# Taking the four key blocks of a causal attention in the order 0, 3, 1, 2

## What is computed

```python
q = q * cos + _rotate_half(q) * sin
k = k * cos + _rotate_half(k) * sin
scores = jnp.einsum('bqhd,bkhd->bhqk', q, k) / jnp.sqrt(jnp.float32(D))
causal = jnp.tril(jnp.ones((T, T), dtype=bool))
scores = jnp.where(causal, scores, jnp.float32(-1e+30))
p = jax.nn.softmax(scores, axis=-1)
y = jnp.einsum('bhqk,bkhd->bqhd', p, v).reshape(B, T, C)
```

## Time and profile before

| | |
|---|---|
| timed runs, median of 3 | 347.4 us (345.73, 347.4, 354.85) |
| the profiled execution | 344.2 us; its span in the profile 342.4 us |
| PE busy | 317.1 us (93%) |
| DVE busy | 248.9 us (73%) |
| ACT busy | 216.5 us (63%) |
| POOL busy | 127.7 us (37%) |
| causal attention, steps 0 to 31 | about 107 to 187 us |

### The profile page before, as it was taken

One profiled execution on the slowest core, in us unless ns is written; L12 is line 12 of the kernel. 1 busy time (PEld: TensorE's weight loads), 2 busy tenths in 40 slices (PEclk: granted clock), 3 DMA queues, 4 the chain that ended last, 5 costly groups with the idle time before them and its releaser, 6 DMA issues.

```text
span 342.4 us, 6803 instructions
## 1 busy us (share of the span) xinstructions
PE 317.1 (93%) x2270; PEld 221.3 (65%) x2270; DVE 248.9 (73%) x766; ACT 216.5 (63%) x641; POOL 127.7 (37%) x183
## 2 busy tenths in 40 slices
PE   8799989998989999997999998998999899999886
PEld 2348778664544333354544998995678687878675
DVE  4988875884889999988352563379787867888476
ACT  1488885374466755564378664764776576676995
POOL 3455563110732444403231360410685525545400
PEclk9999999999999999998799999999999999999999
DMA  7590000086752520090002003100100000000002
GB/s 210 192 278 5 2 0 2 9 264 173 208 190 72 138 74 3 11 351 15 2 17 71 2 23 101 50 0 0 56 17 17 1 2 0 3 0 0 2 0 64
DMA packets 21881, 22.47 MB, mean 66 GB/s; under 512 B 3894, under 2 KB 18646, under 8 KB 21846
## 3 DMA queue, kind: packets, MB, share of 16 engines
q1 hardware_dynamic: 18982, 16.78, 17.0%
q10 hardware_dynamic: 2352, 4.20, 3.8%
q0 software_dynamic: 512, 1.05, 1.0%
HBM read 14.22 MB, written 7.60 MB: 64 GB/s over the span
## 4 chain that ended last, share of the span: by engine, by line
PE 57%; DVE 17%; ACT 13%; issue 5%; POOL 4%; DMA 3%; SPq 0%; ACTq 0%; POOLq 0%
PE PS L1388 51%; PE PS L1442 5%; DVE PS L873 5%; ACT big L1176 5%; ACT big L1364 3%; POOL big L529 2%; DVE big L691 2%; DMA big<-in_A_WkT 2%; DVE big L716 2%; ACT big L1306 1%; DMA XN<-scr_y,pos 1%; ACT big L1150 1%; DVE XN L668 1%; POOL big L531 1%; DVE mraw L705 1%
## 5 line engine op out<-in xcount | busy, mean ns | idle before, releaser
L1388 PE MATMUL PS<-big 128*128 128x128 f32 (+10 forms) x592 | 94.6, 311 | 9.1 <-DVE mB L873 4.1
L1388 PEld LDWEIGHTS PS<-big 128*128 128x128 f32 (+3 forms) x592 | 56.4, 151 | 42.9 <-DVE mB L873 21.3
L529 POOL TENSOR_TENSOR big<-big,urec 128x1024 f32<-128x1024 f32 x24 | 45.6, 1898 | 60.2 <-DVE urec L723 45.5
L1176 ACT ACTIVATE big<-big 128x154 f32<-128x154 f32 x192 | 60.5, 318 | 10.9 <-DVE big L691 5.6
L873 DVE CUSTOM_DVE_ANT_0 PS<-PS,later 128x128 f32<-128x128 f32 (+3 forms) x128 | 59.9, 516 | 8.8 <-PE PS L1388 7.6
L1306 ACT ACTIVATE big<-PS 128x1024 f32<-128x1024 f32 (+3 forms) x64 | 42.8, 701 | 31.1 <-PE PS L1388 31.1
L1150 ACT ACTIVATE big<-PS 128x1280 f32<-128x1280 f32 (+2 forms) x30 | 32.3, 1087 | 27.0 <-PE PS L1442 24.5
L1388 PE MATMUL PS<-kkC,XT 128*128 128x462 f32 (+1 forms) x96 | 36.0, 511 | 2.2 <-DVE big L716 2.2
L517 POOL TENSOR_TENSOR rstd<-ve,minus_half 128x4 f32<-128x4 f32 (+2 forms) x13 | 13.2, 1016 | 61.8 <-DVE ve L663 61.8
L1176 ACT ACTIVATION_READ_ACCUMULATOR big<-big 128x1 f32 x192 | 36.1, 188 | 0.0
L1388 PEld LDWEIGHTS PS<-vwCm,big 128*128 128x128 f32 x256 | 30.9, 192 | 3.9 <-ACT big L1150 1.3
(11 more groups left out here) (193 smaller groups left out, 507.0 us busy)
## 6 DMA issues: line engine op xcount, KB each, us to landing
scr_qk<-big SPq DMA_DIRECT2D x12, 384.0 KB, 3.3
big<-scr_qk SPq DMA_DIRECT2D x16, 288.0 KB
big<-in_wv ACTq DMA_DIRECT2D x1, 2048.0 KB, 8.0
scr_x<-zrow SPq DMA_DIRECT2D x2, 448.0 KB, 6.4
scr_y<-big SPq DMA_DIRECT2D x2, 448.0 KB, 3.5
X<-in_x ACTq DMA_DIRECT2D x2, 256.0 KB, 3.4
big<-in_A_WoT ACTq DMA_DIRECT2D x1, 512.0 KB, 4.7
cw<-in_C_Wk SPq DMA_DIRECT2D x1, 512.0 KB, 5.3
```

The lines of the kernel that those rows point to most:

```text
L529: pool.tensor_tensor(pn[:, 0:GH * P].rearrange("p (h k) -> p h k", h=GH), Pt[u % 3][:, :, 0:KM], r.to_broadcast([P, GH, KM]), ALU.mult).th ...
L1176: i = act.activation(Pt[u % 3][:, h, :], Pt[u % 3][:, h, :], ACT.Exp, accum_out=usum[:, u % 3, h:h + 1])
L1388: return pe.matmul(o, lhsT, rhs, start=start, stop=stop)
```

## The change

The key blocks of each group are taken in the order 0, 3, 1, 2. Everything that went by kt as a place in the group (the first block, which starts the accumulation and waits; the last, which ends it) now goes by `at`, the place; everything that went by kt as a block (widths, slices) goes by `KEY_ORDER[at]`.

```diff
+        KEY_ORDER = (0, 3, 1, 2)
...
             for n in range(B * 4 * QT * 2):
                 s, pair = divmod(n, 2)
-                w = T - P * (s % QT)
+                w = T - P * KEY_ORDER[s % QT]
...
             def outputs(s):
 
-                bg, kt = divmod(s, QT)
+                bg, at = divmod(s, QT)
+                kt = KEY_ORDER[at]
...
-                if kt == 0 and bg:
+                if at == 0 and bg:
                     pe.wait_ge(yg_ready, bg)
                 for j in range(4):
                     i = mm(PS[32 * j:32 * j + 32, AV_BANK, kt * P:T], vaug[:, b, kt, 4 * g + j, :],
-                           PTb[:, 4 * ((s + 1) % 2) + j, 0:T - kt * P], start=kt == 0, stop=kt == QT - 1)
+                           PTb[:, 4 * ((s + 1) % 2) + j, 0:T - kt * P], start=at == 0, stop=at == QT - 1)
...
-                g, kt = divmod(step, QT)
+                g, at = divmod(step, QT)
+                kt = KEY_ORDER[at]
                 w = T - kt * P
-                if kt == 0:
+                if at == 0:
                     pe.wait_ge(m_ready[s // QT % 2], 16 * 3 * (s // QT // 2 + 1))
```

## The result

The kernel with the order 0, 3, 1, 2 takes 1.0061 times as long as before, with an interval of 1.0037 to 1.0085. This ratio leaves out the executions in which TensorE's clock was low for long (10 of 22 with the change, 3 of 22 before); the medians of all executions are 350.88 us (347.23 to 361.97) against 346.92 us (344.46 to 354.85), a ratio of 1.0114, and without those executions they are 348.5 against 346.6. A second comparison on another chip gave 1.0060 (1.0031 to 1.0088), with 345.86 us against 343.83 us. So the change costs some 2.1 us of 345 (0.0060 x 345), where the forecast was 350.2 us, 2.8 more than before. The range, 344.7 to 353.6 us, held the result, and it lies within the 2% that was given 91 in 100. The path behind the number was not all as forecast, and its errors partly offset each other.

What follows compares the result with a forecast made beforehand. PE and DVE, both near full, bound the first sequence; PE alone bounds steps 17 to 20. Terms 1.3 + 0 + 0.4 + 1.1 = 2.8 us, added to 347.4, gave 350.2 us; range 344.7 to 353.6.

Steps and rivals of the forecast that it cites:

- place 0: First step of a first-sequence group (kt 0): O 0.64 for 0.42, hidden by the mask; cost 0, or 0.21 uncovered.
- places 1 and 2: Second and third steps of a first-sequence group: kt 3 for kt 1, gain 0; kt 1 for kt 2, cost 0.12.
- place 3: Last step of a first-sequence group: O of kt 1, 0.85 for 0.64, right before the next S; cost 0.21.
- first sequence: Four groups, each 0.33 us longer: 1.3 us in all, bounds 0.4 and 2.2.
- steps 16 to 20: Start of the second sequence: PE is the bound and its sums of S and O stay the same; 0.
- steps 20 to 27: Second sequence, forecast as steps 21 to 27: longer S of step 23 and O of step 22 behind the logits; +0.4.
- steps 28 to 31: End of the attention: wider last steps and ACT's weight copies delay the last O; +1.1 us, bounds 0.3 and 1.4.
- the three signs: Group repeats in 9.5 us or less; clock row has another number of low slices; stage after step 31 changes length.
- Place 1: Second step of a first-sequence group, kt 3 for kt 1: S 0.24 shorter, O waits for the mask; gain 0.
- the clock stays up: Rival at step 21's wait: the stall no longer brings the clock's fall, 3.4 us come back, 346.8 us; 10 in 100.
- The second fall: Rival in steps 24 to 31: TensorE's clock falls once more, 3.4 us added, 353.6 us; 12 in 100.

Runs made afterwards that it cites:

- the control: The kernel before, unchanged, timed and profiled again beside itself; ratio 1.0016 (0.9986 to 1.0046).
- the first sequence alone: Against the kernel before: order 0, 3, 1, 2 in the four groups of the first sequence only; 344.06 us, 1.0016 (0.9989 to 1.0042).
- the whole change: The changed kernel as it is, order 0, 3, 1, 2 in both sequences, compared again with the kernel before; 345.86 us, 1.0060 (1.0031 to 1.0088).

## Why the prediction came out as it did

| term | forecast | measured | |
|---|---|---|---|
| place 0, a group | 0 | +0.07 | by DVE's copy, not named in the prediction |
| places 1 and 2, a group | 0 + 0.12 | +0.11 | |
| place 3, a group | +0.21 | +0.21 | |
| first sequence | 4 x 0.33 = 1.3 | 3 x 0.39 = 1.2 | group 0 costs nothing |
| steps 16 to 20 | 0 | +0.35 | |
| steps 20 to 27 | +0.4 | +0.83 + 0.11 = +0.94 | |
| steps 28 to 31 | +1.1 | +0.76 | |
| sum at the same clock | 2.8 | 3.24 | bounds were 0.7 and 4.1 |
| the clock | 0 (rival: -3.4) | about -1 | in executions without a long fall |

The median of 350.88 lies near the forecast of 350.2 by luck: the forecast is for an execution without a long fall of the clock, and those have a median of 348.5. The base of the forecast was high for such executions as well, 347.4 where they have 346.6. What can be held against the forecast is the difference, 2.8 for a measured 2.1, and the terms above. Of the three signs that were to show the prediction wrong, the first did not come (9.85 us, not 9.5 or less). The second did: the clock row has one low slice in place of two, but so has the control, so it is a matter of the execution. The third, the length behind step 31, was met in a small way only (155.3 for 155.6 and 155.8), apart from the profile taken with the result.

**The first sequence: size right, mechanism named wrongly.** The step that failed is "that O waits for the mask, which does not depend on it". O of kt 0 waits for DVE's copy of the last group's outputs (`yg_ready`); the runs without the masks and with a short copy show it. The two end 0.13 us apart, the trace names the mask, and the prediction took it at its word, although the kernel has `pe.wait_ge(yg_ready, bg)` in plain sight at that very place, in the diff even; the list of waits ahead of the prediction lacks it too. The sum survived by luck: the copy depends on the change only weakly, and the error of 0.07 in each of three groups was less than the 0.33 wrongly charged for group 0. Place 1, gain 0, held for a similar reason: the copy does not come earlier for a narrower S. PE's ring product ahead of O does, 2.93 behind S in place of 3.12, and PE then waits 0.24 us for the copy. (The 0.24 of the prediction's place 1 should have been 2 x (0.17 - 0.07) = 0.20 by its own prices.)

**Steps 16 to 20: the step that failed is "the sums are the same", so 0.** PE's work is the same, 10.5 to 10.6 us busy, but it is no longer without a gap. The S of step 17 is now 0.43 shorter (before, the four matmuls of 384 took 4 x 0.17, now 4 x 0.06 of 128), while O of kt 0 behind it stays where the copy puts it: 3.80 behind S of step 16, where it was 3.73. PE waits 0.25 us there, and the other 0.10 of the 0.35 stands as busy time. It is the argument made for place 1 of the first sequence, that a gain ahead of a fixed wait is lost, and it was not carried over: where work moves from before a fixed wait to behind it, an equal sum is a loss.

**Steps 20 to 27: mis-sized, 0.94 for 0.4.** What was forecast is there: step 23 takes 1.72 in place of 1.30 us, behind the logits. Not in the sum were step 20, 2.54 in place of 2.33, which is O of kt 2 in place of kt 3, 0.21 longer, ahead of the wait of step 21, and 0.18 in steps 21 and 22 together. The prediction weighed the O of place 0 in the first sequence and forgot it here, where the wait of step 21 follows. That wait, of the changed kernel:

```profile
162.36 0.39 PE L1389 MATMUL PS<-big 72*128 72x384 bf16 x2 [2.15 <-DVE mB L874]
```

It is 2.15 us as in the earlier trace rows: it moved as a whole, and was no cover for what stands before it. The remaining 0.11 of steps 24 to 28 was forecast as 0.

**The end: mis-sized the other way, 0.76 for 1.1.** The walk was right in its order and in the wait for ACT before the last O, 6.10 us for a forecast of 6.2 behind the second pair of step 29. But it started from the same S of step 28 and the same first exponential. ACT's first exponential of step 28 starts 0.76 us behind S there, where it was 0.98, and the second pair of step 29 therefore 2.75 behind it, in place of 2.96 (179.89 to 182.64; the earlier profile has 181.59 - 178.63). A walk has to start where both kernels are alike on both engines; ACT was not.

**The clock gave about 1 us back.** In eleven of the twelve profiles the clock falls near the end of the wait of some 2 us in step 21, from 0.9 us before it to 1.8 us behind it, and comes back after 3.4 or 6.8 us; in the profile of the first sequence alone it does not fall there. As steps 20 to 24 are the same in that kernel, in the control and in before, they price the fall: 12.27 us without it, 13.63 with the short one and 14.93 with the long one, so 1.36 and 2.66 us. The three long falls began 0.3 to 0.9 us before the wait ended, the short ones from 0.04 before to 1.8 behind; no run tests whether that decides. The mean granted clock of an execution tells how long the clock was low in all, though not where: of the profiles at 0.995, before again and the whole change have one short fall in step 21, the first sequence alone one in group 0. At 0.995 the changed kernel has a median of 345.6 us and the kernel before 342.27, 3.3 apart, close to the 3.24 of the traces. But before has 0.995 in 5 of 35 executions and 0.99 in 17, the changed kernel 0.995 in 7 of 12 and 0.99 in 2. So the comparison of medians sees 2.1 of the 3.3. The rival "the clock stays up" had the place right and the size wrong: it took 3.4 us as what can come back, where the whole fall costs 2.66 and the common case is the step between its two lengths, 14.93 - 13.63 = 1.30. Before was profiled in its common case, and after too, so the profiles differ little: spans of 342.4 and 344.0.

**The second fall,** a rival with 12 in 100 for steps 24 to 31, did not come there in any profile. But a long fall came in the first sequence, in the profile taken with the result:

```profile
PE 330.1 (92%) x2270; PEld 225.4 (63%) x2270; DVE 249.7 (69%) x766; ACT 216.6 (60%) x641; POOL 127.7 (36%) x183
PEclk9999999999996555999899999999999999999999
```

The same groups that took 9.85 us took up to 15.34 there, and the work of the other engines was the same. The Trainium skill ("TensorE: Matmul & The Clock Gate", section "A second HAM failure mode: psum-queue depth-cycling") has small idle times between matmul groups, with PSUM banks cycled in between, as enough for such a swing. Most traces here do not agree: groups with the same waits ran at 1.00. Some do fall, and what sets one execution apart from another is open. Executions with a mean clock of 0.975 or less were 10 of 22 and 3 of 12 with the changed kernel, together 13 of 34. With the kernel before they were 2 of 12, 2 of 35 and 3 of 24, and by their times, as no clock was kept there, 3 of 22: together 10 of 93. That speaks for a link with the order, and so for a cost that the ratio of 1.0061 leaves out; but no experiment tested it, and the counts of the other kernels (3, 4, 3 and 1 of 12) do not settle it.

## What to carry to other kernels

Where two engines hand work to each other, an order of steps is not worth its evenness: 0, 1, 3, 2 is as uneven as the order of before and has the shortest group (9.21 us), while 0, 3, 1, 2 and 0, 2, 1, 3, with the evenest sums, have the longest (9.85 and 9.78); what counts is which piece stands just ahead of a hand-over that somebody waits for, and which piece falls in front of a wait that does not move, where a gain is lost. Write down all the waits of an instruction with the times at which they end, and the time at which its own engine is free for it, not only what the profile names; where two are within 0.2 us take each away in turn, and then both. Before a small difference is trusted, compare executions with the same mean granted clock: here it hid a third of the loss.

## What the chip showed that was not expected

- Near the end of the same wait of 2.15 us, with the same instructions in steps 20 to 24, the clock falls for 3.4 us, for 6.8 us or not at all, and steps 20 to 24 take 13.63, 14.93 or 12.27 us.
- A start on PE that waits for a DVE copy is 0.14 to 0.15 us behind the copy's end, and the releaser that a row names was not always the one that counted: "[0.24 <-POOL big L608]" stands where the mask of this O had ended 0.35 us before and the copy 0.15, and "[0.72 <-ACT big L1307]" where the copy had ended 0.15 before.
- A fill of 1.42 us on ACT, behind a step's exponentials, turned a gain of 0.25 us in a group into a loss of 0.32.
